# State-space groups: another order of the projection tiles, the mask behind the scaling, and the square sums of two batches side by side

## What is computed

```python
proj = input_states @ in_proj_w.T          # gate (8192), x (8192), B and C (8 groups of 128), dt (128)
conv = conv_general_dilated(xBC, conv_w, (1,), [(K - 1, 0)], feature_group_count=CONV)   # 4 taps
xBC = silu(conv + conv_b)                  # the gate has no convolution
y = _ssd(hs, A, Bm, Cm, D, dt, dt_bias)    # scan over chunks of tokens
g = y * silu(gate)
gg = g.reshape(b, l, G, GS)                # 8 groups of 1024 channels
var = mean(gg * gg, axis=-1, keepdims=True)
g = (gg * rsqrt(var + EPS)).reshape(b, l, INTER) * norm_w
return g @ out_w.T
```

## The profile before, and how to read it

| what | value |
|---|---|
| profiled execution, span | 2281.85 us, 2279.9 us |
| mean granted TensorE clock | 0.976 |
| busy: TensorE, weight loads | 2129.2 us (93%), 1566.7 us (69%) |
| busy: VectorE, ScalarE, GpSimd | 1468.0 (64%), 1319.6 (58%), 866.0 us (38%) |
| state-space part, start-up | 544 to 619 us |
| its groups 0 to 7 | 619 to 1892 us |
| output stage | 1896 to 2280 us |

### The profile page before, as it was taken

One profiled execution on the slowest core, in us unless ns is written; L12 is line 12 of the kernel. 1 busy time (PEld: TensorE's weight loads), 2 busy tenths in 40 slices (PEclk: granted clock), 3 DMA queues, 4 the chain that ended last, 5 costly groups with the idle time before them and its releaser, 6 DMA issues. The chain is left out here.

```text
span 2279.9 us, 37039 instructions
## 1 busy us (share of the span) xinstructions
PE 2129.2 (93%) x12040; PEld 1566.7 (69%) x12040; DVE 1468.0 (64%) x1813; ACT 1319.6 (58%) x2368; POOL 866.0 (38%) x758
## 2 busy tenths in 40 slices
PE   6889999888999999899999998998999986999998
PEld 5644444567777777677777776776777754888886
DVE  4546666265487877776687686785777654555555
ACT  2145555434577887687678678677778762222332
POOL 0011111130166756566575565565666660000000
PEclk9989999999999999999999999999999997999999
DMA  3422222231454554444444445444435556444462
GB/s 132 161 75 73 78 71 58 77 124 56 124 161 136 168 176 138 153 137 154 134 149 156 146 155 160 130 138 157 151 126 177 168 162 240 140 142 140 143 215 74
DMA packets 184023, 310.81 MB, mean 136 GB/s; under 512 B 20496, under 2 KB 96784, under 8 KB 183712
## 3 DMA queue, kind: packets, MB, share of 16 engines
q1 hardware_dynamic: 183840, 308.53, 42.9%
HBM read 252.52 MB, written 55.68 MB: 135 GB/s over the span
## 5 line engine op out<-in xcount | busy, mean ns | idle before, releaser
L145 PE MATMUL ssm_pp<-xhi,ssm_lo 128*128 128x512 f32 x1192 | 483.8, 406 | 44.8 <-issue 25.8
L147 PE MATMUL ssm_pp<-xhi,ssm_hi 128*128 128x512 f32 x1192 | 470.5, 395 | 0.0
L146 PE MATMUL ssm_pp<-xlo,ssm_hi 128*128 128x512 f32 x1192 | 470.4, 395 | 0.0
L1412 ACT ACTIVATE ssm_sct<-ssm_cumb,ssm_gpar 128x128 f32<-128x128 f32 x1024 | 313.0, 389 | 105.0 <-DMA ssm_cumb<-dt_sums 94.6
L145 PEld LDWEIGHTS ssm_pp<-xhi,ssm_lo 128*128 128x128 f32 x1192 | 227.1, 190 | 111.6 <-issue 51.5
L137 POOL TENSOR_TENSOR ssm_lo<-ssm_raw,ssm_hi 128x512 fp32r<-128x512 f32 x149 | 249.1, 1678 | 93.5 <-ACT ssm_hi L126 93.3
L1513 DVE SCALAR_TENSOR_TENSOR ssm_xc<-ssm_pp,vectors,ssm_xc 128x1022 f32<-128x1022 f32 (+2 forms) x192 | 245.0, 1276 | 46.8 <-ACT ssm_xc L1373 32.0
L1548 DVE TENSOR_TENSOR ssm_sct<-ssm_sct,ssm_cbm 128x1024 f32<-128x1024 f32 x128 | 227.3, 1776 | 70.3 <-ACT ssm_sct L1419 52.7
L147 PEld LDWEIGHTS ssm_pp<-xhi,ssm_hi 128*128 128x128 f32 x1192 | 227.1, 190 | 49.5
L146 PEld LDWEIGHTS ssm_pp<-xlo,ssm_hi 128*128 128x128 f32 x1192 | 227.6, 191 | 44.3
L1560 DVE TENSOR_TENSOR ssm_xp<-ssm_turn,ssm_gpar 128x512 f32<-128x512 f32 x128 | 87.7, 685 | 225.5 <-PE ssm_turn L1268 218.6
(11 more groups left out here) (210 smaller groups left out, 3986.2 us busy)
## 6 DMA issues: line engine op xcount, KB each, us to landing
ssm_cumb<-dt_sums SPq DMA_DIRECT2D x96, 1024.0 KB, 6.6
ssm_raw<-w SPq DMA_DIRECT2D x149, 256.0 KB, 2.7
gated<-ssm_go SPq DMA_DIRECT2D x128, 256.0 KB, 5.1
out_graw<-gated SPq DMA_DIRECT2D x64, 512.0 KB, 4.1
out_raw<-w SPq DMA_DIRECT2D x65, 256.0 KB, 2.6
ssm_cumb<-dt_sums SPq DMA_DIRECT2D x32, 512.0 KB, 4.7
ffn_raw<-w SPq DMA_DIRECT2D x37, 256.0 KB, 2.8
stk_qs<-qk_parts SPq DMA_DIRECT2D x96, 64.0 KB, 2.2
```

The costliest lines, as they stand in the source:

```text
L145: pe.matmul(out, wlo, xhi, start=start, stop=False)
L146: pe.matmul(out, whi, xlo, start=False, stop=False)
L147: return pe.matmul(out, whi, xhi, start=False, stop=stop)
L1412: i = act.activation(sct[:, s % 2, h, :], cumb[:, s % 2, 0, h, :], ACT.Relu, scale=-1.0, bias=gpar[:, unit, 0, s % NTOK, h:h + 1])
```

## The change

Five edits. (1) `ENTRIES`: of the first half, g1 comes before x0, and g2 behind x3 (before: g0, x0, x1, g1, g2, x2, x3, g3; after: g0, g1, x0, x1, x2, x3, g2, g3). The weights are laid out by this list. (2) `AT`: entries spread differently; steps 3 and 10 have two tiles (before steps 2, 9 and 11), and step 15 has g3, "products" and "turn B" (before, "products" was in step 14, and step 15 had only "turn B"). `SILU_START` and `SILU_END` follow, and GpSimd does the `low` of step 15's tile at the next step 0. (3) `mask` stands behind `scaled`. (4) `squares` sums both batches at steps 3 and 11 alone, batch b into PSUM partitions 32b to 32b + 31; one copy of 64 partitions instead of two of one. (5) Each batch's row goes out by a DMA of its own, for unit 1 at step 5 instead of 9; the semaphore counts follow.

```diff
-ENTRIES = ["B", "C", "g0", "x0", "x1", "g1", "g2", "x2", "x3", "g3", "products", "turn B",
+ENTRIES = ["B", "C", "g0", "g1", "x0", "x1", "x2", "x3", "g2", "g3", "products", "turn B",
            "x4", "x5", "g4", "g5", "x6", "g6", "x7", "g7"]
...
-        AT = [(12,), (13,), (14, 15), (16,), (17,), (18,), (19,), (20,), (21,), (22, 23), (24,),
-              (25, 26), (27,), (28,), (29, 30), (31,)]
-
-        SILU_START = {3: (15, 12, 13), 5: (17, 16), 7: (19, 18), 10: (20, 21), 12: (26, 23, 24), 15: (27, 28)}
-        SILU_END = {2: 14, 9: 22, 11: 25, 14: 29}
+        AT = [(12,), (13,), (14,), (15, 16), (17,), (18,), (19,), (20,), (21,), (22,), (23, 24),
+              (25,), (26,), (27,), (28,), (29, 30, 31)]
+
+        SILU_START = {3: (14, 12, 13), 5: (17, 16), 7: (19, 18), 10: (22, 20, 21), 13: (24, 25), 15: (28, 26, 27)}
+        SILU_END = {3: 15, 10: 23, 15: 29}
...
-            return g * 4 + (s // NC - 2) if s >= NTOK or not isinstance(g, int) or g > 0 else 0
+            return g * 2 + s // NTOK
...
-                sp.wait_ge(var_done, g * 4 + (unit * 2 + 2))
-                sp.dma_start(c.var_dram[unit, bass.ds(g, 1), :], sqs[0:1, unit, :]).then_inc(var_out, 16)
+                sp.wait_ge(var_done, g * 2 + (unit + 1))
+                for b in range(B):
+                    sp.dma_start(c.var_dram[unit, bass.ds(g, 1), b * L:(b + 1) * L],
+                                 sqs[32 * b:32 * b + 1, unit, 0:L]).then_inc(var_out, 16)
...
-            def squares(b, unit):
-
-                mm = pe.matmul(p_state[0:32, :], c.ones[:, 0:32], sqs[:, unit, b * L:(b + 1) * L],
-                               start=True, stop=True)
+            def squares(unit):
+
+                for b in range(B):
+                    mm = pe.matmul(p_state[32 * b:32 * b + 32, :], c.ones[:, 0:32], sqs[:, unit, b * L:(b + 1) * L],
+                                   start=True, stop=True)
                 mm.then_inc(var_sum, 1)
...
-                    if ch == 0 and (summed or s == NTOK):
+                    if s % NTOK == NC and summed:
                         after(pe, var_done, var_before(g, s))
...
-                elif summed:
+                elif summed and s % NTOK < NC:
                     pe.wait_ge(state_done, g * NCA + carried(s))
                     pe.wait_ge(sqs_done, g * NS + (0 if s < NTOK else NTOK))
-                    squares(s % NTOK // NC, unit)
+                    squares(unit)
...
-            def copy_squares(k, unit, b):
-
-                act.wait_ge(var_sum, k * 2 + (b + 1))
-                act.activation(sqs[0:1, unit, b * L:(b + 1) * L], p_state[0:1, :], ACT.Copy).then_inc(var_done, 1)
+            def copy_squares(k, unit):
+
+                act.wait_ge(var_sum, k + 1)
+                act.activation(sqs[0:32 * B, unit, 0:L], p_state[0:32 * B, :], ACT.Copy).then_inc(var_done, 1)
...
-                    if s == NS - 1 and not last:
-                        mask(g + 1)
                     for e in AT[s - 1][-1:] if s else ():
                         if is_conv(e) and (e < NE or not last):
                             conv(g, e)
                     if behind(g, s, 1, last):
                         scaled(*behind(g, s, 1, last))
+                    if s == NS - 1 and not last:
+                        mask(g + 1)
...
+                    for e in AT[NS - 1] if s == 0 and before(g, 0, 1) else ():
+                        if is_tile(e):
+                            low(real(g - 1, e, AHEAD))
```

More of the change, by code:

```diff
@@ L1183, in body @@
                         squares_out(g - 1, 0)
-                    if s == 9 and before(g, 0, 1):
+                    if s == 5 and before(g, 0, 1):
                         squares_out(g - 1, 1)
@@ L1195, in body @@
                     if last and s == 10:
-                        sp.wait_ge(var_out, 2 * (G - 1) * 16)
+                        sp.wait_ge(var_out, 2 * (G - 1) * B * 16)
                         for unit in range(2):
@@ L1213, in _ @@
             sp.wait_ge(pre_out, NPRE * 16)
-            sp.wait_ge(var_out, 2 * G * 16)
+            sp.wait_ge(var_out, 2 * G * B * 16)
         @block.tensor
@@ L1351, in _ @@
             pe.wait_ge(sqs_done, G * NS)
[L1352 to L1355, removed]
+            pe.wait_ge(var_done, G * 2 - 1)
+            squares(1)
         @block.scalar
@@ L1466, in body @@
                     if s % NC == 0 and s % NTOK > 0 and (s > NTOK or before(g, 0, 1)):
[L1467 to L1471, removed]
+                        copy_squares(g * 2 - 1 + s // NTOK, 1 - s // NTOK)
                     for e in SILU_START.get(s, ()):
@@ L1494, in _ @@
             passes(act, body)
-            copy_squares(2 * G - 2, 0, 1)
             square(G - 1, NS - 2)
             square(G - 1, NS - 1)
-            copy_squares(2 * G - 1, 1, 0)
-            copy_squares(2 * G - 1, 1, 1)
+            copy_squares(2 * G - 1, 1)
         @block.vector
@@ L1686, in add_squares @@
                 if t == 0:
-                    after(pool, var_out, g * 32 - (16 if s == 0 else 0))
+                    after(pool, var_out, g * 64 - (32 if s == 0 else 0))
                 pool.wait_ge(sqa_done, n + 1)
```

## The result

The changed kernel takes 2264.18 us, the median of four runs (2260.67 to 2265.07), against 2284.59 us for the kernel before (2281.54 to 2290.81, four runs): ratio 0.9907, 95% interval 0.9889 to 0.9926.

A forecast was written before the change was run, and what follows sets the result against it. The state-space part was taken as bound by TensorE's matmul stream. Terms -13.6 - 2.3 - 6.0 + 3.5 + 12.8 = -5.6 us gave 2276.3 against the profiled 2281.85, or 2281 on the runs' median; range 2265 to 2297.

The forecast's parts named there:

- The pair: Square sums on TensorE: a pair side by side costs 0.97 to 1.00 us, as one sum did before.
- The last sum: Tail: the last two square sums become one pair, 2.3 us less.
- The waits for convs: TensorE's waits before projection tiles and "products" in the reordered part: 12.5 us fall by 6.0 us.
- The mask: Mask behind "products" at the loop's edge: 0.35 us shows at each of two edges without a jump, 0.7 us more.
- The start-up: Before tile 6, TensorE waits for x1's late weight, high, tap, conv and copy: 12.8 us more, 10.4 to 15.
- The jumps themselves I leave as they are: Loop's edge: the jumps' cost stays unchanged; bounds, nothing to 5 x 2.3 us less if the clock stayed up.
- Rival 4: Loop's edge: jumps get cheaper by shorter work after the last outputs or a clock staying up; 11.4 us less, 2270; 8%.
- Turn B's wait: Loop's edge: turn B waits 0.4 us for the SiLU of g3 at each of 7 edges, 2.8 us more.
- rival 1: Loop's edge: turn B waits in every group for g3's SiLU behind Exp; slower, 2294 or 2300; 14%.
- +10 for the one: New order of tiles, with mask and start-up: -6.0 + 3.5 + 12.8, an increase of 10 us.
- -16 for the other: Square sums in pairs: 13.6 us less in the stream and 2.3 in the tail, 16 us less.
- The 13.6 us for the square sums: TensorE's stream: 14 sums of 0.97 us go, 13.6 us less.

The follow-up runs named there:

- The thin load: Kernel before, with the broadcast load for step 1 of groups 1 to 7 cut to one head of eight (128 KB instead of 1 MB): 2265.33 us against 2282.83.
- the extra copy: Changed kernel plus an unneeded 1 MB copy within device memory, issued by SyncE at each group's end: 2277.61 us in one run.
- the kernel with the start-up put right: Changed kernel with tap ahead of high, turns and copies behind entry 3, and SyncE's table writes at entry 7: 2251.26 us, later 2251.03.
- the fastest version: The kernel with the start-up put right, plus ScalarE's SiLU of g3 ahead of the Exp in step 15: 2245.95 us against 2251.03 without.

## Why the prediction was wrong

**Right.** The pair costs 0.98 us and stands at steps 3 and 11 alone; sixteen of them. The last sum gives 2.4 us (2.3 forecast). The waits for convs fell by 6.4 us (6.0), with the 1 us before g3's tile and none before "products". The mask shows 1.0 us at the edges without a jump (0.7). The start-up slips by the chain that the forecast wrote down; 12.8 us against 16.1 in the profiled run and 14.0 in the mean of five profiles with this start-up, inside its bounds of 10.4 to 15 as a mean, though the profiled run is outside them.

**The step that failed** is the sentence "The jumps themselves I leave as they are". The five jumps cost 10.6 us less idle time and 3.5 us less low clock. The forecast took the 4.87 us behind "issue" for a constant of the jump. It is a fetch, and the fetch begins only as the 1 MB load that SyncE issued 1.5 us ahead of the jump is nearly through; the edit put "products" and turn B, 2.8 us of matmuls, ahead of the jump, which now stands 5.8 us behind that load. The rows that would have said so were there: the five waits before differed, 4.3 to 5.8 us, which a constant doesn't, and the DMA share in the 3 us from the jump on was 0.97. The thin load and the extra copy show it from both sides, -16.5 and +12.6 us of span. Rival 4 had the right sign and the right place, but its reasons were the clock and the work behind the outputs, and its bound of 11.4 us came from the clock alone; it got 8% where the rows would have borne much more.

**The term that wasn't there.** Turn B's wait was put at 2.8 us. TensorE never waits for it: turn B begins 0.65 us behind the SiLU's end (slack forecast: 0.4 us). But the chain Exp, table load, SiLU did become what the edge hangs on, in a way that rival 1 didn't see: it holds the jump instruction in the queue. Putting the SiLU ahead gave 5.1 us. The drain of 1.38 us that the Trainium skill gives for a switch of table sets ("ScalarE: Activation LUTs", What ACT_TABLE_LOAD costs) doesn't show here: Exp begins 1.29 us after its load begins (1249.94 and 1251.23), and the SiLU 1.29 us after its own (1252.31 and 1253.60).

**Two terms off in opposite directions.** The new order alone saves 13.7 us, the pairs alone 5.7, and both together 20.4, so the measured parts add up. The forecast had +10 for the one and -16 for the other. That its sum of -5.6 has the right sign and misses the range by under 1 us is luck: one part was 24 us too high, the other 10 too low. The 13.6 us for the square sums left the stream as forecast, but a matmul saved in front of a fetch that waits for other transfers, or of a conv for which TensorE waits anyway, saves little. At step 7 it was kept, at step 15 it was not.

## What to carry to other kernels

An idle time with "issue" at a loop's edge was no constant here: look at what the DMA engines carry in the 3 us around the jump, at when the packet of the instruction queue begins, and at what the jump instruction itself waited for in its queue, which the matmuls' own waits don't show. Work that needs no new data belongs between the last large load and the jump, and the last instruction with a semaphore wait ahead of the jump should have its wait over early. Before a saving in the stream is multiplied by its count, check at each place whether TensorE waits for something else right behind it.

## What the runs showed of the hardware

A jump that is taken cost TensorE 3.5 to 7.4 us in these kernels; at the end of the last pass, in the kernel with the start-up put right, the same instruction, not taken, lasted 83 ns. Its duration went with the traffic around it: median 7.02 us at 0.6 us behind the issue of the 1 MB load, 6.28 at 1.5, 4.31 at 5.8, 4.22 at 6.4, and 3.84 at 1.5 with the load cut to an eighth. The distance is not all of it: 4.28 at 5.3 with the SiLU first, 4.64 at 5.8 without. Of a jump's duration the stretch from the end of its fetch was 1.3 to 1.6 us everywhere, the fetch 0.9 to 2.2, and the wait before it 0.9 to 5.1; nearly all of the difference between the kernels lies in this wait. The Trainium skill, page "Runtime: NRT & Kernel Launch" (Instruction fetch mechanics), says that a taken branch whose target lies outside the two pages at hand forces a DMA fetch before execution goes on. These runs agree, by the packet in queue q8 behind each jump, and add what the page doesn't say: that the fetch waits for the kernel's own transfers, by about 3 us (7.02 against 3.84).

Behind an idle time of 2.51 us the first 4 us of the next tile had a mean granted clock of 0.57 in the kernel after, so most of them ran at the lower level, 1.2 GHz; behind 4.87 us in the kernel before it was 0.50, that level throughout; and behind 2.37 us with the new order alone 1.00, the upper level, 2.4 GHz. The rows, in this order, have the clock third from the end:

```profile
1258.82:1262.82 4.00, 4.00 (x11) 3.13 (x12) 2.35 (x5) 3.98 (x11) 0.00 (x0) 0.57 0.15 38
1257.76:1261.76 4.00, 4.00 (x10) 3.13 (x11) 0.83 (x3) 2.63 (x6) 2.26 (x3) 0.50 0.89 272
1256.38:1260.38 4.00, 3.99 (x18) 3.31 (x19) 2.35 (x5) 3.98 (x12) 0.34 (x1) 1.00 0.21 66
```

An idle time of 2.5 us didn't always lead to a slow tile: with the new order alone two tiles behind waits of 2.95 and 2.37 us took 5.57 us, and a third behind 2.27 us took 7.18. In the fastest version all five took 7.16 to 7.20 us behind 2.2 to 2.6 us.
